# Attention and a feed-forward layer on one core: sums of weighed heads spread through DRAM, shifts on GpSimd, v copied by ScalarE

## The reference

```python
x = hidden_states                                 # (16, 512, 512)
x = x + layernorm(attention(layernorm(x)))
x = x + layernorm(feed_forward(layernorm(x)))
# attention:
q, k, v = (split_heads(h @ W.T + b) for W, b in ((Wq, bq), (Wk, bk), (Wv, bv)))
q, k = apply_rope(q, freqs), apply_rope(k, freqs)
scores = where(causal, q @ k.T / sqrt(16), -inf)
out = softmax(scores) @ v                         # per head
return merge_heads(out) @ Wo.T + bo
```

## Time and profile before

| | us |
|---|---|
| median of 3 runs | 2745.22 (2744.34 to 2745.78) |
| profiled execution | 2745.2 |
| its span | 2743.5 |
| TensorE busy in the span | 2519.6 |
| VectorE busy | 2122.0 |
| ScalarE busy | 1419.8 |
| GpSimd busy | 983.8 |

### The profile page before, as it was taken

The page is one execution under the profiler, slowest core; times in us unless marked ns, Lnnn a source line. Parts: engine busy times, 40 slices in busy tenths (PEclk is TensorE's granted clock), DMA queues, the critical chain, the costliest instruction groups (busy, mean ns, idle before and its releaser), DMA issues. The chain is left out here.

```text
span 2743.5 us, 55677 instructions
## 1 busy us (share of the span) xinstructions
PE 2519.6 (92%) x19584; PEld 1213.8 (44%) x19584; DVE 2122.0 (77%) x6399; ACT 1419.8 (52%) x1838; POOL 983.8 (36%) x1083
## 2 busy tenths in 40 slices
PE   3899999999999999999999996099999999999997
PEld 1444544444454454454454443044444444444443
DVE  5999999999999999999999994735555455555454
ACT  3576776776766666767676664322222222222221
POOL 4454655655565565555556553000000000000000
PEclk8999999999999999999999999599999999999999
DMA  5332433433333433433442330401121111121111
GB/s 170 98 95 76 125 92 99 122 104 94 115 105 92 117 104 92 121 102 95 123 118 77 106 96 32 191 16 46 46 76 46 46 61 46 46 76 46 46 46 46
DMA packets 125314, 236.66 MB, mean 86 GB/s; under 512 B 11441, under 2 KB 94897, under 8 KB 111921
## 3 DMA queue, kind: packets, MB, share of 16 engines
q1 hardware_dynamic: 123056, 232.84, 27.8%
q10 hardware_dynamic: 2048, 1.05, 0.1%
HBM read 148.39 MB, written 84.41 MB: 85 GB/s over the span
## 5 line engine op out<-in xcount | busy, mean ns | idle before, releaser
L655 DVE CUSTOM_DVE_ANT_0 mx<-mx,causal 128x512 f32<-128x512 f32 (+3 forms) x2048 | 944.3, 518 | 47.4 <-PE mx L785 43.4
L491 ACT ACTIVATE probs<-ts,exp_scale 128x1024 f32<-128x1024 f32 x640 | 708.8, 1107 | 325.7 <-PE ts L799 323.7
L1229 DVE SCALAR_TENSOR_TENSOR hidden<-gu,up_scale,silu 128x512 f32<-128x512 f32 x176 | 131.9, 750 | 417.7 <-PE gu L1279 407.9
L1088 ACT ACTIVATE silu<-gu,gate_scale 128x512 f32<-128x512 f32 x176 | 120.9, 687 | 631.4 <-PE gu L1279 631.4
L1063 POOL TENSOR_TENSOR f_rstd<-f_var,f_neg_half 128x4 f32<-128x4 f32 x32 | 32.3, 1009 | 928.8 <-DVE f_var L1206 647.3
L403 POOL TENSOR_SCALAR_AFFINE_SELECT probs<-probs 128x512 f32<-128x512 f32 x512 | 311.7, 635 | 145.2 <-ACT probs L491 145.2
L1277 PE MATMUL gu<-f_xT_hi,gate_hi 128*128 128x512 f16 x704 | 268.0, 381 | 51.9 <-issue 51.9
L813 PE MATMUL xb<-probs,vs 128*32 128x512 f32 (+3 forms) x4096 | 305.5, 439 | 5.0 <-ACT shift_rows L497 3.0
L382 POOL TENSOR_TENSOR turned<-biased,sin_sb 64x512 f32<-64x512 f32 x128 | 170.0, 1328 | 327.3 <-ACT biased L476 320.9
L655 DVE DVE_READ_ACCUMULATOR2_ANT row_max<- 128x1 f32 x2048 | 285.5, 139 | 0.0
L1279 PE MATMUL gu<-f_xT_lo,gate_hi 128*128 128x512 f16 x704 | 267.8, 380 | 0.0
(11 more groups left out here) (148 smaller groups left out, 4469.3 us busy)
## 6 DMA issues: line engine op xcount, KB each, us to landing
slots<-half SPq DMA_DIRECT2D x260, 128.0 KB, 12.6
qT<-slots SPq DMA_DIRECT2D x128, 256.0 KB, 3.8
kT<-slots SPq DMA_DIRECT2D x128, 256.0 KB, 4.0
xn<-x SPq DMA_DIRECT2D x16, 1024.0 KB, 9.1
xr<-x SPq DMA_DIRECT2D x16, 1024.0 KB, 6.9
slots<-half SPq DMA_DIRECT2D x256, 64.0 KB
x<-xr SPq DMA_DIRECT2D x16, 1024.0 KB, 10.8
f_xn<-x SPq DMA_DIRECT2D x16, 1024.0 KB, 4.8
```

The source lines that it names most:

```text
L491: nc.scalar.activation(probs[:, g % 2, u, :, :], ts[:, :, :], ACT.Exp, scale=exp_scale[:, 0:1]).then_inc(ts_read, 1)
L655: last = nc.vector.tensor_tensor_reduce(out=scores, in0=scores, in1=causal[:, T - P * (qt + 1):T], scale=1.0, scalar=-3e38, op0=ALU.add, o ...
```

## The change

Three things change. First, `oT` is no longer transposed twice. SyncE writes it to DRAM (`send_weighed`, 256 KB a group). For each pair of groups it fetches two tiles (`fetch_weighed`): `averaged`, the 8 heads' 16 rows packed to 128 partitions, and `sums`, the row of sums of each head repeated 16 times. VectorE takes the reciprocal of all of `sums`, 128x512, GpSimd multiplies, ScalarE adds v's bias (which commutes with the average) and rounds, VectorE takes the rest. Second, the shift is computed by GpSimd in three instructions and placed by SyncE. Third, v is copied by ScalarE, without bias. The cosine now reads PSUM and adds the bias itself, and it frees the bank of queries and keys. With fewer uses, the banks are dealt out anew.

```diff
-        TURNED = (("x", 2, 1), ("x", 3, 1), ("a", 3, -1), ("a", 0, 0), ("x", 0, 2), ("a", 1, 0), ("x", 1, 2), ("a", 2, 0))
+        TURNED = (("x", 2, 1), ("x", 3, 1), None, None, ("x", 0, 2), None, ("x", 1, 2), None)
+        AVERAGED = {0: (2, -1), 2: (3, -1), 4: (0, 0), 6: (1, 0)}
+        FETCHED = {1: (3, -1), 3: (0, 0), 5: (1, 0), 7: (2, 0)}
-        STATISTICS_AT = {14: (0, 1), 15: (2, 3)}
+        STATISTICS_AT = {15: (0, 1), 16: (2, 3)}
...
-        BANK_USES = []
+        BANK_USES, r = [], 0
         for g in range(NG):
-            r = g % 2
-            BANK_USES += [(("qk",) + QUERIES_KEYS[g], r), (("s", (g + 1) % NG, (g + 1) // NG), 1 - r), (TURNED[g], r),
-                          (("av", (g - 1) % NG, (g - 1) // NG), 1 - r), (("o", (g - 1) % NG, (g - 1) // NG), 1 - r),
-                          (V_OR_OUT[g], r)]
+            BANK_USES += [(("qk",) + QUERIES_KEYS[g], r), (("s", (g + 1) % NG, (g + 1) // NG), 1 - r)]
+            if TURNED[g]:
+                BANK_USES.append((TURNED[g], 1 - r))
+                r = 1 - r
+            BANK_USES += [(("av", (g - 1) % NG, (g - 1) // NG), 1 - r), (V_OR_OUT[g], r)]
+            r = 1 - r
...
-        FREED_BY = {"qk": (biased_ready, 8), "v": (v_read, NC), "out": (out_read, NT), "s": (shift_read, NG),
-                    "av": (oT_ready, NG), "o": (o_read, NG), "a": (aT_ready, NC), "x": (xT_ready, NC)}
+        FREED_BY = {"qk": ((cosine_done, 8),), "v": ((v_read, NC),), "out": ((out_read, NT),),
+                    "s": ((shift_read, NG),), "av": ((oT_ready, NG),), "x": ((xT_ready, NC),)}
...
+            def place_shift(i, g):
+                sp.wait_ge(shift_read, turned_rows)
+                wait_if_any(sp, shift_in, placed)
+                for pair in range(2):
+                    sp.dma_start(qT[SHIFT_ROWS, g // 2, 2 * (g % 2) + pair, :],
+                                 shift_rows[4 * pair:4 * pair + 4, g % 2, :]).then_inc(shift_in, 16)
+
+            def send_weighed(i, g):
+                sp.wait_ge(oT_ready, ready)
+                wait_if_any(sp, averaged_in, fetched)
+                sp.dma_start(weighed[g // 2, g % 2, :, :], oT[:, :]).then_inc(weighed_out, 16)
+
+            def fetch_weighed(i, c):
+                sp.wait_ge(weighed_out, 16 * (NG * i + 2 * c + 2))
+                wait_if_any(sp, aT_ready, consumed)
+                heads = weighed[c, :, :, :].rearrange("g (h r) t -> (g h) r t", r=32)
+                sp.dma_start(sums[:, :], heads[:, DH:DH + 1, :].broadcast_to([8, DH, T])).then_inc(averaged_in, 16)
+                sp.dma_start(averaged[:, :], heads[:, 0:DH, :]).then_inc(averaged_in, 16)
...
+                    if u == 4 and exists(i + (g - 1) // NG):
+                        send_weighed(i + (g - 1) // NG, (g - 1) % NG)
                     if u == 1 and exists(i + owner):
                         send_slots(i + owner, n)
-                    if u == 2 and exists(i + owner):
+                    if u == 1 and g in FETCHED:
+                        c, of = FETCHED[g]
+                        if exists(i + of):
+                            fetch_weighed(i + of, c)
+                    if u == 2 and exists(i + (g + 1) // NG):
+                        place_shift(i + (g + 1) // NG, (g + 1) % NG)
+                    if u == 3 and exists(i + owner):
                         fetch_slots(i + owner, n)
-                    if s == 8 and exists(i + 2):
+                    if s == 9 and exists(i + 2):
...
+            def shift_of_maxima(i, g):
+                pool.wait_ge(mx_read, NS * i + NU * (g + 1))
+                wait_if_any(pool, shift_full, NG * i + g)
+                nc.gpsimd.tensor_scalar(shift[:, :, :, :, 0], row_max[:, g % 2, :, :, :], -1.0 / SHIFT_UNIT, None,
+                                        ALU.mult).then_inc(shift_step, 1)
+                nc.gpsimd.tensor_scalar(row_shift[:, :, :, :], row_max[:, g % 2, :, :, :], -1.0 / SHIFT_UNIT, None,
+                                        ALU.mult).then_inc(shift_step, 1)
+                pool.wait_ge(shift_step, 2 * (NG * i + g + 1))
+                nc.gpsimd.tensor_tensor(shift[:, :, :, :, 1], row_shift[:, :, :, :], shift[:, :, :, :, 0],
+                                        ALU.subtract).then_inc(shift_ready, 1)
+
+            def average(i, c):
+                pool.wait_ge(averaged_in, 32 * (NC * i + c + 1))
+                pool.wait_ge(recip_done, NC * i + c + 1)
+                nc.gpsimd.tensor_tensor(averaged[:, :], averaged[:, :], sums[:, :], ALU.mult).then_inc(averaged_done, 1)
...
+            def high_of_attention(i, c):
+                act.wait_ge(averaged_done, NC * i + c + 1)
+                nc.scalar.activation(aT_hi[:, (NC * i + c) % (NC + 2), :], averaged[:, :], ACT.Identity,
+                                     bias=bias_v[:, c:c + 1]).then_inc(aT_hi_done, 1)
...
+            def reciprocal_of_sums(i, c):
+                dve.wait_ge(averaged_in, 32 * (NC * i + c + 1))
+                nc.vector.reciprocal(sums[:, :], sums[:, :]).then_inc(recip_done, 1)
+            def low_of_attention(i, c):
+                nc.vector.scalar_tensor_tensor(aT_lo[:, place, :], averaged[:, :], bias_v[:, c:c + 1], aT_hi[:, place, :],
+                                               ALU.add, ALU.subtract).then_inc(aT_ready, 1)
             def cosine(i, n):
-                nc.vector.tensor_tensor(roped[:, n % 2, :], biased[:, n % 2, :], cos_sb[:, :],
-                                        ALU.mult).then_inc(cosine_done, 1)
+                nc.vector.scalar_tensor_tensor(roped[:, n % 2, :], xb[:, bank_of("qk", n), :], bias_qk[:, which, ct:ct + 1],
+                                               cos_sb[:, :], ALU.add, ALU.mult).then_inc(cosine_done, 1)
```

More of the change, by code:

```diff
@@ L417, in body @@
                     n, owner = QUERIES_KEYS[g]
+                    ahead, due = divmod(s + AHEAD - NU, NS)
+                    if u == 0 and exists(i + ahead):
+                        before = shift_of_maxima(i + ahead, due // NU)
                     if u == 0 and exists(i + (g - 1) // NG):
@@ L422, in body @@
                         before = add_turned(i + owner, n)
+                    if u == 1 and g in AVERAGED:
+                        c, of = AVERAGED[g]
+                        if exists(i + of):
+                            before = average(i + of, c)
                     if u == 4 and exists(i):
@@ L442, in _ @@
             body(1)
-            with pool.Fori(2, NB - 2) as i:
+            for i in range(2, NB - 2):
                 body(i)
@@ L729, in body @@
                             low_of_roped(i + owner, n)
-                    if u == 3 and exists(i + (g - 1) // NG):
-                        divide_by_sums(i + (g - 1) // NG, (g - 1) % NG)
                     if exists(i + 2):
@@ L825, in turn_shift @@
                 last.then_inc(shift_full, 1)
-            def turn_weighed(i, g):
-                bank = bank_of("o", g)
-                pe.wait_ge(oT_ready, NG * i + g + 1)
-                for t in range(NT):
-                    last = nc.tensor.transpose(xb[:, bank, P * t:P * (t + 1)], oT[:, P * t:P * (t + 1)], ident[:, :])
-                last.then_inc(o_full, 1)
             def turn_x(i, c, bank):
@@ L839, in turn_x @@
                 last.then_inc(xT_full, 1)
-            def turn_attention(i, c, bank):
-                pe.wait_ge(o_read, NG * i + 2 * c + 2)
-                for t in range(NT):
-                    last = nc.tensor.transpose(xb[:, bank, P * t:P * (t + 1)], attn[:, c % 2, t, :], ident[:, :])
-                last.then_inc(aT_full, 1)
             def project_queries_keys(i, n, owner, part):
```

148 lines of the change are left out of this document (70 added, 78 removed).

## The result

| | before | after |
|---|---|---|
| median, us | 2745.16 (2744.34 to 2745.78, 4 runs) | 2930.91 (2924.64 to 2937.39, 4 runs) |
| ratio to before | 1 | 1.0677 (95% interval 1.065 to 1.0704) |
| span of the profiled execution | 2743.5 | 2932.8 |
| mean granted TensorE clock over the span | 0.977 | 0.948 |

The changed kernel is 186 us slower. The forecast was +19, its range ended at +105. From one load of a sequence's x to the next it takes 111.3 us (mean of 13), against 100.9 before: 10.4 more. In the profiled executions the attention phase is 188 us longer (the feed-forward phase's first load is issued at 1719.8 before and 1908.2 after). 164 of them are lost by the write of x issued at 1618.1 before and 1782.1 after, the other 24 behind it, in the last sequence.

The account below looks back on a forecast made before the run. TensorE was taken to set the pace, VectorE nearly as full; afterwards stalls behind four reciprocals a sequence were to decide. 2745 + 8 (101.6 against 101.1 us, 15 sequences) + 11 (tail) = 2764 us, range 2685 to 2850.

Parts of the forecast that it names:

- The lump's length: VectorE's reciprocal of 128x512, four a sequence: 3.1 us each, extrapolated from rows of 1, 4 and 16 elements.
- The rival with eight cycles: VectorE's reciprocal takes eight cycles an element, 4.4 us each: 78 us slower, 2842; chance 0.04.
- the one that priced it like an addition: VectorE's reciprocal takes 0.68 us, so TensorE sets 92.5 us a sequence: 2627; chance 0.06.
- The heads' fetch: SyncE's fetch ahead of the reciprocal: due after 7.9 us, lands after about 7.5, hidden by 0.4; group 3's 1.2 late.
- the late-fetch rival: The heads' fetch delays the reciprocal; one us in each pair of groups costs 60 us: 2824; chance 0.15.
- The shift's transfer: On SyncE behind both fetches, it lands about when its scores start; TensorE is idle then, so no cost.
- the forecast's own walk: From reciprocal to reciprocal, two groups each: 25.5 + 25.5 + 25.8 + 24.8 = 101.6 us a sequence against 101.1.
- The coupling of weighing to the cosine: In groups 0, 1, 4, 6 weighing needs a bank the cosine frees; waits of 1 to 2 us in 0, 4, 6.
- VectorE's sum: VectorE's work a sequence: 98.7 - 12.9 - 3.3 + 0.5 + 12.4 = 95.4 us, about 6 below today's period.
- GpSimd's shifts: Eight shifts of three small operations, about 1 us together, placed where GpSimd waits for ScalarE.
- The tail: Before the last tile's projection: write, fetch, reciprocal, product and rounding take 13.4 us against 2.2 today, +11 us.
- the three signs given for being wrong: Lumps below 2 us; VectorE's waits for scores under 2 us a sequence; or each reciprocal waiting for its transfer.

Follow-up runs that it names:

- both transfers moved: Changed kernel with the heads' fetch issued in unit 0 instead of 1 and the shift transfers issued by ScalarE: 2912.9 us; with a minimum replacing the reciprocal, 2729.14.
- The early fetch: Changed kernel with the fetch of the averaged heads issued in unit 0, ahead of the slot writes, instead of unit 1: 2882.21 us, ratio 1.0496.
- the short lump in place: Changed kernel with the 128x512 reciprocal replaced by an elementwise minimum of the same size, sums not inverted, nothing else touched: 2830.46 us, ratio 1.0308.
- both with the shift moved: Changed kernel with heads' fetch in unit 0, a minimum in place of the reciprocal, and shift transfers issued by ScalarE: 2729.14 us, ratio 0.9941.
- the shift moved alone: Changed kernel with only the shift transfers issued by ScalarE again instead of SyncE: 3029.81 us, ratio 1.1033.

## Why the prediction was wrong, point by point

**The sign was right, the size was not**: +19 forecast, +186 measured, above the range. The steps:

- *The lump's length.* 3.1 taken, 3.35 measured (3.3 was the upper bound). Four times 0.25 is 1.0 us a sequence, 15 us of the 167 missed. The rival with eight cycles has fallen: it put the lump at 4.4. So has the one that priced it like an addition. That each us of lump is a us of the sequence was too dear for the kernel as it stands: 0.6 was measured there, 1.1 with both transfers moved.
- *The heads' fetch, the first step that failed.* It was put at "hidden by 0.4", once 1.2 late. It is waited for in 26 of 29 pairs, up to 2.9 us, 6.4 a sequence. The estimate took the page's 3.8 us to landing of another fetch and a little more "behind others"; around 1045 it took 7.2 from the second issue. That the slot writes ahead make it slow isn't shown: in the last sequence, with none in flight, it still takes 6.1 us (issued at 1866.58, reciprocal at 1872.69), though a write of x of 1 MB is issued 1.2 us behind it. That `sums` reads each row 16 times is a rival that no run separates. The 12.6 us of the earlier trace rows, which the late-fetch rival leaned on, don't bear on it: they are of four writes in the first 13 us of the program, the only ones of this group with a landing on record. The early fetch gives 49 us back (with the shift's transfer earlier too), so the rival had the right mechanism and too small a chance, 0.15. Its price (1 us late in each pair is 60) was too high: the wait is 1.6 us a pair, which would be 95.
- *The shift's transfer, the second.* It was costed at nothing because "TensorE has idle time there". It had, but this idle time was the forecast's own, behind the lump; the wait is at another place, ahead of it, and adds 7.4 us a sequence to TensorE's waits. What it costs the program isn't shown: the runs that took this wait out were slower or no different as long as the reciprocal stood at full length or in quarters.
- *The clock, the third.* The forecast took every product at the durations of before, at a granted clock of 1.00. In the forecast's own walk TensorE stands idle behind each lump, and in the trace weighing behind such idle time takes up to 4.06 us in place of 2.36, in 5 of 57 groups. The granted clock is 0.96 in 1000 to 1500, with only two levels, one half the other, so 8% of this time, 9 us a sequence, is at the lower one. Products there start 0.43 us apart and not 0.22 (below, in the tail), so that is at most 4.5 of the 10.4 us, an estimate. The Trainium skill describes such a clock in "TensorE: Matmul & The Clock Gate", section "Part 1: The HAM clock gate": the clock has two levels and falls to the lower after idleness. The trace agrees, with 0.73 us busy in 3.5 and 0.58 granted after it. It belonged in the forecast, by this bound as a smaller term than the waits.
- *The coupling of weighing to the cosine* was seen and is there (2.83 us at 1058.57, 1 to 2 were forecast). Taking it out gives 47 us. What was missed is that the late fetch ahead of the lump and, in some groups, the slow clock behind it add to it. From the start of the reciprocal to the end of weighing the walk had 10.6 us; in this pair it is 13.4, of which 1.7 is the clock, 0.8 the low half and 0.2 the lump.
- *VectorE's sum.* The cosine is 0.74 (0.75 taken). But `half`, not in the change, went from 754 ns in the mean (the same view of before) to 816, with 1.57 us where it stands beside both of GpSimd's sine products (1054.34). The sum was to fall by 3.3 us; measured, VectorE's busy time a sequence is the same as before, 96.5 against 96.4. Over 93% busy was forecast, 87% came, so the sum did not set the pace.
- *GpSimd's shifts* at no cost: right. They take 0.26, 0.25 and 0.22 us, and with v's copy they are a gain of 12 us.
- *The tail.* +11 forecast, from terms that add to 14.3 and not to the 13.4 given, so it should have been +12. The last weighed heads are copied by 1863.9 and the first projection of the last tile starts 15.1 us later, against 2.2 before: +13. After this pause the projection's first 18 products run at about half the speed; they start 0.43 us apart and not 0.22, another 4 us:

```profile
1879.04 0.61 PE L823 MATMUL xb<-w_hi,aT_hi 128*128 128x512 f16 x1 [13.93 <-DVE aT_lo L702]
1879.44 0.63 PE L824 MATMUL xb<-w_lo,aT_hi 128*128 128x512 f16 x1
1879.87 0.63 PE L825 MATMUL xb<-w_hi,aT_lo 128*128 128x512 f16 x1
...
1889.21 0.38 PE L823 MATMUL xb<-w_hi,aT_hi 128*128 128x512 f16 x1
1889.43 0.38 PE L824 MATMUL xb<-w_lo,aT_hi 128*128 128x512 f16 x1
```

The sum failed in its form as well. It walked from lump to lump and let each new wait vanish in the idle time that the walk had found. The runs show the waits in series: late transfer, lump, cosine, at times slow weighing, then VectorE short of scores. Nor do their prices add up. The early fetch alone gives 49, the short lump in place 100, both with the shift moved 202, the shift moved alone -99. Of the three signs given for being wrong, "each reciprocal waits for its transfer" is the one that came true.

How much of the 186 us belongs to the clock alone isn't separated: the bound of 4.5 us a sequence above is all there is. The run that kept weighing at full speed did so with 96 us of added work.

## What to carry to other kernels

Price an operation that comes in one piece by what stands behind it on its engine and by who frees whose buffer there. How much of it comes back when it is made short depends on the other waits: 0.6 us for each us here, 1.1 with the transfers moved. If several rows of a tile are copies of one another, invert before spreading and not after. Where a wait on TensorE makes a pause of some microseconds, the products behind it can run at half speed, as in 5 of 57 groups here and in 20 of 53 with the shift on ScalarE. And a transfer's time to landing is to be taken from a row of the same form at the same place in the queue, looking at what the row counts; if there is none, it is a range and not a number.

## What the runs showed of the hardware

- VectorE's reciprocal, whole tile in SBUF: 0.346 us for 32 elements a partition, 0.945 for 128, 3.353 for 512. Both steps give 6.2 to 6.3 ns an element, and some 0.14 us are fixed. An estimate from rows of 1, 4 and 16 elements was 8% too low.
- The repeat count of eight that the Trainium skill gives for this divide ("VectorE: DVE Perf Modes", the 8-slice pipeline) isn't eight cycles an element here: at the page's 0.96 GHz 6.27 ns are six.
- The lower level of TensorE's clock: weighing 4.06 us after 3.5 us with 0.73 busy, 2.36 in 52 of 57 groups. More work for TensorE (some 96 us of transposes ahead of weighing) cost 9 us, raised the mean granted clock from 0.947 to 0.957 and left no weighing of 59 slow, where 10 of 59 had been.
- Moving two small transfers from one engine's queue to another changed the time by +99, +31, +2 (within the spread of the runs) and -8 us in four versions of the same kernel. The sign of such an edit isn't a property of the edit.
